# Splitting the experts' weights: none in iterations 8 and 9, eleven pieces in each of the others

## What is computed

```
x = x + einsum(fp8_round(layernorm(x)), fp8_round(ctx))     # per batch, 512 x 512 x 512
x = x + layer(layernorm(x)):
    h = rmsnorm(hidden); q, k, v = projections (16 query heads, 4 key heads, width 128)
    q, k = rope(rmsnorm(q)), rope(rmsnorm(k)); causal softmax attention; o projection; residual
    router: softmax over 8 experts, two best; y = sum of their weight * wd(silu(wg t) * wu t)
```

## Time and profile before

| | us |
|---|---|
| median of 3 runs | 1408.67 |
| lowest and highest | 1400.69, 1410.27 |
| profiled execution, its own time | 1403.31 |
| its span | 1401.5 |
| mean granted clock of TensorE | 0.966 |

### The profile page before, as it was taken

How to read it: one execution, slowest core, us unless ns; L and a number is a source line. 1 busy time by engine, 2 the same in 40 slices (tenths; PEclk the granted TensorE clock), 3 DMA queues, 4 the chain that set the end, 5 groups by cost and what they waited for, 6 DMA issues and landing times. The chain is left out here.

```text
span 1401.5 us, 22860 instructions
## 1 busy us (share of the span) xinstructions
PE 1256.1 (90%) x6845; PEld 1012.2 (72%) x6845; DVE 841.9 (60%) x2480; ACT 715.9 (51%) x2290; POOL 384.1 (27%) x545
## 2 busy tenths in 40 slices
PE   1767899999999999978999999999997499999995
PEld 0456667787776777757767778778775398988995
DVE  7667776766887686568777665666644422222221
ACT  5446665564765566466656656556543133333331
POOL 0223221232422132223213222342210124333331
PEclk9988899999999999999999999999998599999998
DMA  3270325422355466637554764765304797877433
GB/s 98 73 286 24 121 106 181 173 110 109 151 148 186 149 221 199 233 103 216 182 181 144 244 208 153 231 221 193 103 3 122 273 327 213 241 217 203 77 61 38
DMA packets 89895, 228.50 MB, mean 163 GB/s; under 512 B 12273, under 2 KB 50033, under 8 KB 79537
## 3 DMA queue, kind: packets, MB, share of 16 engines
q1 hardware_dynamic: 63712, 184.03, 37.5%
q0 software_dynamic: 10848, 24.71, 9.5%
q10 hardware_dynamic: 15216, 18.30, 3.7%
HBM read 146.76 MB, written 80.24 MB: 162 GB/s over the span
## 5 line engine op out<-in xcount | busy, mean ns | idle before, releaser
L535 POOL TENSOR_TENSOR prob<-prob,rtotal 128x128 f32<-128x128 f32 (+2 forms) x192 | 118.1, 620 | 418.6 <-DVE rtotal L1294 392.5
L957 ACT ACTIVATE prob<-prob,bias 128x128 f32<-128x128 f32 (+3 forms) x256 | 144.9, 566 | 152.1 <-DVE prob L1288 151.2
L1288 DVE TENSOR_SCALAR_CACHE_REDUCE prob<-bank,nscale 128x128 f32<-128x128 f32 (+3 forms) x256 | 134.6, 543 | 140.0 <-PE bank L713 139.7
L677 PE MATMUL bank<-w_hi,hT_hi 128*128 128x512 f32 x480 | 175.3, 365 | 15.0 <-DVE rot L1253 15.0
L732 PE MATMUL bank<-pT,v 128*128 128x512 f32 (+3 forms) x512 | 175.7, 445 | 9.0 <-ACT pT L963 8.3
L963 ACT ACTIVATE pT<-bank 128x512 f32<-128x512 f32 (+3 forms) x256 | 102.9, 432 | 127.8 <-PE bank L721 127.6
L677 PE MATMUL bank<-w_hi,hT_lo 128*128 128x512 f32 x480 | 163.7, 341 | 0.0
L677 PE MATMUL bank<-w_lo,hT_hi 128*128 128x512 f32 x480 | 163.6, 341 | 0.0
L1598 PE MATMUL gu<-we,xT_hi 128*128 x624 | 156.5, 332 | 4.1 <-DVE xT_lo L1714 2.7
L512 POOL TENSOR_TENSOR r<-r,rot 128x640 f32<-128x640 f32 x60 | 100.2, 1670 | 186.5 <-DVE rot L1253 186.5
L711 PE MATMUL bank<-kT_hi,qT_hi 128*128 128x128 f32 (+3 forms) x256 | 101.2, 395 | 22.2 <-DVE prob L1288 22.2
(11 more groups left out here) (312 smaller groups left out, 2841.6 us busy)
## 6 DMA issues: line engine op xcount, KB each, us to landing
w_hi<-ws_scratch SPq DMA_DIRECT2D x24, 1024.0 KB, 5.3
w_lo<-ws_scratch SPq DMA_DIRECT2D x24, 1024.0 KB, 7.7
we<-wx_scratch SPq DMA_DIRECT2D x16, 1408.0 KB, 11.0
we<-wx_scratch SPq DMA_DIRECT2D x16, 768.0 KB
stage<-in_wexp SPq DMA_DIRECT2D x64, 176.0 KB, 2.4
wx_scratch<-ehi ACTq DMA_DIRECT2D x64, 176.0 KB, 2.5
wx_scratch<-stage SPq DMA_DIRECT2D x64, 176.0 KB, 2.6
stage<-in_wqkvo SPq DMA_DIRECT2D x40, 256.0 KB, 3.6
```

The source lines that it names most:

```text
L535: nc.gpsimd.tensor_tensor(p, p, rtotal[:, 4 * h + q:4 * h + q + 1].broadcast_to([P, KEYS[q]]), ALU.mult).then_inc(prob_ready, 1)
L677: last = nc.tensor.matmul(o, hT[a][:, k, t * P:(t + 1) * P], wkv(j, c, k) if kv else wq(j, c, k), start=(k == 0 and n == 0), stop=(k == KC ...
L957: nc.scalar.activation(p, p, ACT.Exp, bias=bias[:, 4 * h + q:4 * h + q + 1], scale=-1.0, accum_out=total[:, 4 * h + q:4 * h + q + 1]).then ...
L1288: nc.vector.tensor_scalar(prob[(G * it + h) % (LAG + 1)][:, P_AT[q]:P_AT[q] + KEYS[q]], bank[SC + q % 2][:, 0:KEYS[q]], nscale[it % 2][:, ...
```

## The change

Before, ten places of each iteration from 5 on hold a piece: 5 to 13 hold ten each and 14 the last six. The change adds the place (0, 1), which is the first of the iteration, so that eleven pieces fit in one; it leaves out iterations 8 and 9. Iterations 5 to 7 and 10 to 14 then hold eleven each, and the last eight are in iteration 15, at the places (0, 1) to (2, 2). The 96 pieces, their buffers and their instructions stay the same.

```
-SPLIT_E = [(0, 2), (0, 3), (1, 1), (1, 2), (1, 3), (2, 1), (2, 2), (2, 3), (3, 1), (3, 2)]
+SPLIT_E = [(0, 1), (0, 2), (0, 3), (1, 1), (1, 2), (1, 3), (2, 1), (2, 2), (2, 3), (3, 1), (3, 2)]
 FIRST_E = 5
+E_ITS = (5, 6, 7, 10, 11, 12, 13, 14, 15)
...
-    if it >= FIRST_E and slot in SPLIT_E:
-        m = (it - FIRST_E) * len(SPLIT_E) + SPLIT_E.index(slot)
+    if it in E_ITS and slot in SPLIT_E:
+        m = E_ITS.index(it) * len(SPLIT_E) + SPLIT_E.index(slot)
         if m < NPIECE:
             yield "ew", m
```

## The result

The changed kernel took 1412.81 us in the median of 15 runs (1410.53 to 1421.12), the kernel before 1405.7 us in 15 runs on the same chip (1399.47 to 1410.27). The ratio is 1.0065, 95% interval 1.0047 to 1.0082: some 7 us slower, inside the bound of 1%, but more than the noise. The profiled execution took 1412.99 us, with a span of 1411.2.

A forecast was written before the change was run, and what follows sets the result against it. PE bounds iteration 12 and nearly 9, while iteration 8 also has waits and a slow clock. Terms -3.8 - 1.7 + 3.5 + 1.3 + 0.4 + 3.4 = +3.1 us on a centre of 1406.0 gave 1409.1, range 1399 to 1418.

The forecast's parts named there:

- within 1%: Whole kernel: time changes by no more than one per cent, 14 us; chance 0.85.
- 1.67 and 0.66: Iteration 8: two PE waits in us, standing behind pieces, expected to go entirely once the pieces are removed.
- the twins: Iteration 8: waits of 1.57 and 2.40 us, expected to stay at iteration 4's 1.16 and 1.36 us.
- 65.6 us: Iteration 8 without pieces: predicted length against 69.43, from work, slow clock and the remaining waits.
- its bounds: Iteration 9 without pieces: gain between 0 and 2.9 us, taken as 1.7.
- I take no clock cost: Iteration 5: PE's idle time of about 3 us at (0, 1) leaves the clock high; cost 3.5 us.
- the smaller slower rival: Iteration 5's stand drops the clock, 3.2 us more, and iteration 15 pays its upper bound, 3.6 more: 1415.9; chance 0.14.
- the new store goes out up to 2 us earlier, so the load goes at 802.0 to 804.0: Iteration 11: store at (0, 1) behind save_x2, then the load for (1, 1); cost 0.4 to 2.4, taken 1.3 us.
- The term of the ring: Iteration 7: the three-stage ring delays the piece at (1, 1); cost 0.4 us, bounds 0 and 2.4.
- the rival of a ring that binds in seven iterations: Iterations 6, 7, 10 to 14: late stages cost 2.4 us each, 16.8 instead of 1.7: 1424; chance 0.07.
- The row: Iteration 15: a profiled 8.2 us high store, preferred over the skill's turn-taking rule, by which the cost would be 2.0.
- The reduction comes on time: Iteration 8: rival that a shifted SyncE backlog frees the reduction, saving 3.1 of waiting and 3.2 of clock: 1402.8; chance 0.12.

The follow-up runs named there:

- experiment 1: Changed kernel with the loads of pieces 0 to 2 issued ahead of load_o's 2 MB in iteration 4: 1411.68 us, one run.
- experiment 8: Changed kernel with save_x2's 1 MB store moved to (2, 1) of iterations 7, 11 and 15, timed again: 1406.16 us median of 12, ratio 1.000.
- experiment 6: Changed kernel with load_o(7)'s 2 MB and x's last 1 MB held until POOL's reduction in iteration 8 is done: 1406.53 us, one run.
- experiment 10: Changed kernel with 8 and 9 not emptied: eleven pieces in iterations 5 to 12, eight in 13, none in 14 and 15: 1419.99 us, one run.
- experiment 9: Kernel before, pieces in place, with load_o(7) and x's last 1 MB held until iteration 8's reduction is done: 1399.02 us median of 5, ratio 0.9949.
- experiment 4: Changed kernel with no pieces in 8, 9, 15, ten in 5, 7, 11, fifteen in 12, 13, fourteen in 14: 1425.44 us median of 5, ratio 1.015.
- experiment 2: Changed kernel with save_x2's 1 MB store at (2, 1) of iterations 7, 11 and 15 instead of their start: 1398.17 us, one run.
- experiment 3: Changed kernel with iteration 15's eight pieces at (0, 2) to (2, 3), none at (0, 1): 1408.87 us, one run.
- experiment 11: Changed kernel with ten pieces in 5, 9, 14, eleven in 6, 7, 10 to 13, none in 8, 15; save_x2 at (2, 1): 1402.76 us, ratio 0.9981.
- experiment 5: Changed kernel with x's last 1 MB held until POOL's reduction in iteration 8 is done: 1412.43 us, one run.

## Why the prediction held, point by point

The time of 1409.1 against 1412.8, in the middle of the range's upper half, and "within 1%" are right. The terms are not all so. They were almost all times of waiting, so here each measured change is split into PE's waiting (length less busy time) and PE's busy time, which grows where its clock is low (us, one execution of each kernel):

| iteration | predicted | measured | PE's waiting | PE's busy time |
|---|---|---|---|---|
| 5 | +3.5 | +5.75 | +3.28 | +2.47 |
| 7 | +0.4 | +2.44 | +0.38 | +2.06 |
| 8 | -3.8 | -5.05 | -3.60 | -1.45 |
| 9 | -1.7 | -2.20 | -1.71 | -0.49 |
| 11 | +1.3 | +6.56 | +1.91 | +4.65 |
| 15 | +3.4 | +5.93 | +4.52 | +1.41 |

The waiting was forecast well, four of six terms within 0.3 us. What failed most is that no term had a price for a new fall of the clock.

- **Iteration 8.** The mechanism is right line by line: 1.67 and 0.66 are gone, the twins are at 1.17 and 1.37. "65.6 us" became 64.38. What was left out is PE's busy time, 57.10 before and 55.65 after. Some 0.7 us of it is the clock: by the trace PE worked 5.7 us of the slow stretch before (it took up work at 601.02, the clock rose at 606.7) and 4.4 after (609.32, 613.7). The rest is not traced to an instruction; iteration 9, at the full clock in both, lost 0.49 us of busy time with its pieces too.
- **Iteration 9**, inside its bounds.
- **Iteration 5.** The stand was foreseen to the tenth (ACT at 404.95, "about 405.0"). The step that failed is "I take no clock cost": PE idled 3.36 us and the clock fell. The comparison with the 2.81 us of iteration 4 carried no weight: experiments 1 and 8 show that very wait with the clock falling behind it. It was in the smaller slower rival, at 3.2, and belonged into the forecast. In the seven executions that have this load late, iteration 5 took 73.1 to 75.1 us.
- **Iteration 11.** The place and the queue were right, as the wait for `stage` at (1, 1) shows, and PE's waiting of 1.9 us lies in the bounds of 0.4 to 2.4. Wrong in it was "the new store goes out up to 2 us earlier, so the load goes at 802.0 to 804.0": a store behind 3 MB lands when they have, so going out earlier within them gained nothing. It took 12.07 us instead of 9.99, and the load went 20.5 us into the iteration instead of 19.7, for a piece needed one place sooner. ACT stood 4.48 us, PE 2.15. The larger part, 4.65 us, is the clock, which fell twice, once behind a wait that the kernel before has as well; at the full clock (experiment 6) the iteration cost 1.9 us.
- **Iteration 7.** The term of the ring was right, 0.38 us against 0.4, and 0.6 in experiment 10. The rest is one fall of the clock behind the wait of 1.19 us that every kernel here has in this iteration. It fell behind it in 8 of the 13 profiled executions, experiment 9 with its pieces in the old places among them, so it is no cost of the change that these runs could show.
- **Iterations 6, 10, 12 to 14, nothing predicted.** Right (-0.39, +0.57, 0.0), and so the rival of a ring that binds in seven iterations was rightly small here. It is real, though: experiment 4 met it at fifteen pieces, and experiment 8 in iteration 13 at eleven (56.30 instead of 53.8 us).
- **Iteration 15.** Its pieces without a long wait were put at 2.0 at the least. Experiments 2 and 3 leave 2.8 and 2.7 us, but only 1.4 and 1.3 of it is waiting; the rest is a fall of the clock, which experiment 11 has there with no piece in the iteration. So the 2.0 was too high. ACT's wait for the high store was put at 1.4 and was 3.27 us. Of the Trainium skill's round of turns between queues ("DMA: Bandwidth & Descriptors", section "Queues, rings and completion order") I had said that by it the small store would land in time; it took 5.9 us, ACT's wait is there, and the trace does not agree with it as I had read it. The row decided rightly.
- **The reduction comes on time** did not happen, as argued. Experiments 5, 6 and 9 show its cause, the full DMA engines, and that there was time to be had, in the kernel before (4.3 us of iteration 8, ratio 0.9949) as in the changed one (5.6 us).

The terms that were too small add up to 12.1 us (2.25 + 5.26 + 2.04 + 2.53), those too small on the gaining side to 1.75. The sum of +3.1 was to be +13.6 in the profiled executions and is +7 in the medians. That the medians lie nearer to the forecast is in part luck: the pair of profiled executions overstates the change, because that of before was a draw with a single fall of the clock between iterations 4 and 15, while the same iterations 4, 7 and 11 lost 5.7 us more in experiment 9. I took that one execution for the kernel. The difference is not settled term by term: experiment 8 shows that two executions of one kernel lie 10.9 us apart by where the clock falls and when the reduction ends.

## What to carry to other kernels

A store that a ring waits for lands with the megabytes issued ahead of it on its queue: before adding a user to the ring, move the bulk transfer behind it (iteration 11: 67.3 to 60.8 us). Where one engine's small operation takes twice its time in one iteration, look at what fills the DMA engines then, before thinning out the work around it: the hold of two loads brought more than emptying the iteration did (ratios 0.995 and 0.998). Price every idle time of PE of a microsecond or more with a possible fall of the clock (a stretch of 3.4 us cost 1.6 to 1.7 us here), treat one profile as one draw of these, and before blaming a longer iteration on the change, split it into waiting and busy time and look whether the wait ahead of the fall was there before.

## What the hardware showed that was not expected

- The clock fell behind waits as short as 1.17 us (iteration 11 in experiment 3), and stayed full behind one of 3.19 us (iteration 4 in experiment 4). For one and the same wait it did either, from one execution to the next: behind the wait for the rotation in iteration 4, 2.69 to 3.19 us long, it fell in 7 of 13 executions, and behind the 1.18 to 1.20 us of iteration 7 in 8 of 13. The stretches at 1.2 GHz lasted some 3.5 us, 7 us, and 10 us in two executions (experiments 5 and 8).
- A reduction on POOL, which is no DMA instruction, was held up by the load of the DMA engines: DVE waited 3.00 us for it with idle DMA engines, 4.27 with 2 MB and 6.74 with 3 MB in flight (one execution each; 3.08 and 6.62 us in the kernel before with and without the hold). Through what it is held was not tried.
